# Attention values of two heads in 32 rows of one bank place: half the output copies and transposes, and a new table of steps

## The chip, the cores and the metric

The kernel runs on one core of one Trainium2 chip. The metric is the device time of one launch in microseconds (us). TensorE is written PE in the profile (PEld is its queue of weight loads), VectorE is DVE, ScalarE is ACT, GpSimd is POOL, SyncE is SP.

## The reference, cut to what matters

Two transformer layers over 32 sequences of 256 tokens and 128 channels, all in float32. Each layer is adaptive layer norm, attention with 16 heads of 8 channels, residual, adaptive layer norm, and a mixture of 16 experts of which each token takes two.

```python
h = _layernorm(x) * (1 + ca) + sa
q, k, v = ...                         # 16 heads of 8 channels
scores = q @ k^T / sqrt(8)            # layer 0: + slopes * dist
attn = softmax(scores)
ctx = attn @ v                        # (32, 16, 256, 8) -> (32, 256, 128)
x = x + ga * (ctx @ Wo)
h = _layernorm(x) * (1 + cb) + sb
x = x + gb * experts(h)               # top 2 of 16; layer 1: + a shared expert
```

## The kernel before

**Units and steps.** A unit is one sequence in one layer; there are 64 (32 of layer 0, then 32 of layer 1). The program is one software pipeline over steps, and a new unit enters every 16 steps. Everything a unit needs is placed at a fixed step after the unit's start: `at(step, after)` gives the unit whose step `after` this is. Each engine's program is the same loop over steps (from -44 to about 1280), and within a step it issues what its `if` lines say, in the order of the code. There is no scheduler: each engine's queue is strictly this order, and semaphores do the rest. The last unit enters at step 1008; what follows is the tail.

**A step.** In each step PE computes one head of scores twice: query by key into `ps_s` (L1161, two matmuls), of which DVE takes the row maxima (`mx`, L1553), and key by query into `ps_st` (L1167, two matmuls), of which ACT takes the exponential into `prob` (L821). The first runs at a unit's steps 0 to 15, the second at 26 to 41, with the maxima folded in as extra rows. Both score banks are double: PE's scores of a step wait for DVE's maxima and ACT's exponential of two steps earlier. `prob` holds 8 heads.

**Jobs.** After the scores, PE does at most one or two jobs of `JOBS`, the table of what uses the two banks `ps_job`. Its key is the step modulo 16 (called the place of the step below), and the key's parity is the bank. Before a job, PE waits (`free_bank`) until the last job in that bank has been taken out by DVE or ACT:

```python
for s in range(step - 2, step - 2 * H, -2):
    if standing(s):
        for name, u in standing(s):
            done, value = taken(name, u)
            pe.wait_ge(done, value)
        break
```

**Values.** `av0` to `av3` (`probs_values`, L1032) each take four heads: for each head and each half of the keys, a matmul with the 32 columns of `v_ext` as weights (8 values, a column of ones for the softmax's sum, 23 zeros) and 256 columns of `prob` moving, into rows 32i to 32i+31 of the bank. ACT copies each result of 128 x 256 to `o_sb` (`take_o`, L754). Then `o_t0` and `o_t1` (`out_transpose`, L1040), one for each half of the tokens, transpose four 128 x 128 blocks each, and DVE (`normalise`) takes the reciprocals of the sums (L1372) and multiplies (L1376) into `ctx_sb`. `ctx_t` transposes that, `wo` projects it (L1083), DVE multiplies by the gate (`att_tmp`, L1575), POOL adds it to `x`, DVE and POOL do the second norm (`norm_stats`, `rstd`, `norm_middle` L1342, `norm_rows` L1354), `h2_t` transposes, and `router` (L1097) gives the logits, of which DVE takes the best two (`top_two`).

**Pieces of the experts.** The rows of eight units (a group) are scattered by expert to DRAM by POOL. They are taken in 12 quads of four blocks: transpose (L983), gate and up (L1000, L1001), 10 steps after its start the transpose of the activation (L1013), and 15 after it the down projection (L1020). `QUAD` holds the start step of each: three quads in every 32 steps. POOL gathers the results (`GATHER`) and DVE, ACT and POOL combine them (`COMBINE`).

## Time and profile before

| | us |
|---|---|
| median of 3 runs | 1867.87 (1864.94 to 1874.45) |
| the profiled execution's own time | 1869.03 |
| its span | 1867.3 |
| PE busy | 1491.6 (80%) |
| DVE busy | 1315.7 (70%) |
| ACT busy | 1157.5 (62%) |
| POOL busy | 1028.7 (55%) |
| mean granted clock of PE | 0.911 of full |

A busy share of the whole span mixes stages. The steps of the scores run from about 49 to 1517 us; before is setup, behind is the tail, where no scores are left. In the views, PE is the matmul's own span and PEld the queue from which it is fed, in the program's order, so the start of a job's first weight load and the start of the next thing's first weight load bound the queue time of that job. "Idle before" is the idle time of the engine ahead of an instruction and what ended it. "issue" means nothing that the profile shows was waited for.

### The profile page before, as it was taken

What the parts mean: (1) busy time and instruction counts of PE and PEld (TensorE: products, weight loads), DVE (VectorE), ACT (ScalarE), POOL (GpSimd) and SP (SyncE); (2) the same over time, 40 slices, a digit from 0 to 9 for tenths busy, and PEclk for the clock granted to TensorE, in tenths of its full rate; (3) what the DMA queues carried; (4) which work ended last, traced back from release to release, by engine and by line L of the source; (5) the groups of instructions that cost most, each with busy time, mean ns of one, the idle gap of its engine ahead of it and who ended that gap; (6) DMA issues with size and microseconds to landing.
All of it is one profiled execution on the core that took longest, in us unless ns stands there. A gap on an engine that the chain in (4) does not pass through costs nothing.

```text
span 1867.3 us, 44529 instructions
## 1 busy us (share of the span) xinstructions
PE 1491.6 (80%) x13810; PEld 911.5 (49%) x13810; DVE 1315.7 (70%) x3981; ACT 1157.5 (62%) x2692; POOL 1028.7 (55%) x1411
## 2 busy tenths in 40 slices
PE   2779888889999888899999989998999887435540
PEld 1334444445555555555555555555555555435530
DVE  5669988978888877798888888887788765202110
ACT  1478877877777676677776767766776654113320
POOL 1223335634553766567764767565755556546736
PEclk9989999999999898899999999999999999667665
DMA  6774444445555554455554545555455433224432
GB/s 197 172 205 109 110 103 116 114 122 126 134 130 120 138 132 114 119 127 140 134 137 109 134 122 144 130 124 116 125 134 129 116 87 83 75 80 132 121 93 62
DMA packets 381606, 229.44 MB, mean 123 GB/s; under 512 B 28847, under 2 KB 370161, under 8 KB 380867
## 3 DMA queue, kind: packets, MB, share of 16 engines
q1 hardware_dynamic: 352675, 186.72, 41.4%
q0 software_dynamic: 16384, 33.59, 6.4%
q10 hardware_dynamic: 12320, 6.29, 1.2%
q8 instruction: 120, 1.97, 0.5%
q14 instruction: 107, 0.88, 0.2%
HBM read 122.44 MB, written 103.98 MB: 121 GB/s over the span
## 4 chain that ended last, share of the span: by engine, by line
PE 36%; POOL 20%; DVE 18%; issue 16%; another core or an unknown queue 4%; ACT 4%; DMA 2%; SPq 1%; POOLq 0%; DVEq 0%; ACTq 0%
DVE mx L1553 8%; PE ps_s L1161 7%; POOL y_in L642 7%; PE ps_job L1032 6%; PE ps_q L1020 3%; PE ps_q L1001 3%; POOL slot_dram L625 3%; PE ps_q L983 2%; POOL qk_part L669 2%; POOL y_two L677 2%; POOL qk_rest L665 2%; PE ps_job L1135 2%; PE ps_job L1127 2%; PE ps_q L1013 2%
## 5 line engine op out<-in xcount | busy, mean ns | idle before, releaser
L1553 DVE TENSOR_REDUCE mx<-ps_s 128x2 f32<-128x512 f32 x1024 | 688.2, 681 | 150.3 <-PE ps_s L1161 123.7
L821 ACT ACTIVATE prob<-ps_st 128x512 f32<-128x512 f32 x1024 | 598.9, 593 | 111.1 <-PE ps_st L1167 82.6
L1161 PE MATMUL ps_s<-k_stk,q_stk 51*128 51x256 bf16 x2048 | 403.4, 284 | 79.5 <-DVE mx L1553 37.2
L1167 PE MATMUL ps_st<-q_stk,k_stk 53*128 53x256 bf16 x2048 | 400.2, 281 | 0.8 <-ACT prob L821 0.8
L642 POOL DMA_INDIRECT y_in<-y_dram,slot x256 | 252.4, 986 | 106.7 <-issue 54.6
L1032 PE MATMUL ps_job<-prob,v_ext 128*32 128x256 f32 x4096 | 287.8, 400 | 25.6 <-issue 17.6
L625 POOL DMA_INDIRECT slot_dram<-h_row,slot x256 | 260.6, 1018 | 69.8 <-issue 65.1
L1161 PEld LDWEIGHTS ps_s<-k_stk,q_stk 51*128 51x128 bf16 x2048 | 118.3, 95 | 333.8 <-issue 182.7
L754 ACT ACTIVATE o_sb<-ps_job 128x256 f32<-128x256 f32 x256 | 97.1, 379 | 190.3 <-PE ps_job L1032 127.0
L1032 PEld LDWEIGHTS ps_job<-prob,v_ext 128*32 128x32 f32 x4096 | 115.1, 112 | 133.4 <-issue 54.4
L665 POOL TENSOR_TENSOR qk_rest<-qk_f,qk_part 128x512 f32<-128x512 f32 x64 | 73.9, 1154 | 187.3 <-ACT qk_part L852 187.3
L589 POOL TENSOR_SCALAR ln_ve<-ln_mv 128x2 f32<-128x2 f32 x128 | 28.6, 224 | 225.1 <-DVE ln_mv L1335 219.2
L1541 DVE SCALAR_TENSOR_TENSOR y_two<-y_in,w_top,y_two 128x128 f32<-128x128 f32 x128 | 47.5, 408 | 119.5 <-ACT y_two L736 113.2
L1001 PE MATMUL ps_q<-wgu,h_blk_t 128*128 x640 | 113.1, 310 | 14.8 <-ACT h_blk_t L775 9.7
L1167 PEld LDWEIGHTS ps_st<-q_stk,k_stk 53*128 53x128 bf16 x2048 | 117.0, 95 | 7.9 <-issue 3.8
L1001 PEld LDWEIGHTS ps_q<-wgu,h_blk_t 128*128 128x128 f32 x640 | 95.3, 204 | 24.3 <-issue 22.4
L669 POOL TENSOR_TENSOR qk_part<-qk_rest,qk_part 128x512 bf16<-128x512 f32 x64 | 75.1, 1174 | 53.7 <-ACT qk_part L856 53.0
L983 PE MATMUL ps_q<-ident,h_blk 128*128 128x128 f32 x352 | 66.5, 319 | 43.5 <-issue 30.1
L736 ACT ACTIVATE y_two<-y_in,w_top 128x128 f32<-128x128 f32 x128 | 43.8, 389 | 92.5 <-DMA y_in<-y_dram,slot 58.4
L591 POOL TENSOR_TENSOR ln_rs<-ln_ve,neg_half 128x2 f32<-128x2 f32 x128 | 92.0, 719 | 10.7
L1020 PE MATMUL ps_q<-wd,act_t 128*128 x640 | 97.0, 298 | 0.0
L1020 PEld LDWEIGHTS ps_q<-wd,act_t 128*128 128x128 f32 x640 | 82.8, 202 | 15.0 <-issue 14.7
(206 smaller groups left out, 2919.0 us busy)
## 6 DMA issues: line engine op xcount, KB each, us to landing
part_dram<-qk_part SPq DMA_DIRECT2D x128, 192.0 KB
q_stk<-part_dram SPq DMA_DIRECT2D x128, 192.0 KB
k_stk<-part_dram SPq DMA_DIRECT2D x128, 192.0 KB
h_blk<-slot_dram SPq DMA_DIRECT2D x88, 256.0 KB
y_dram<-y_sb SPq DMA_DIRECT2D x80, 256.0 KB
part_dram<-qk_part SPq DMA_DIRECT2D x128, 128.0 KB
mod_in<-row_dram SPq DMA_DIRECT2D x64, 192.0 KB
part_dram<-qk_part SPq DMA_DIRECT2D x128, 64.0 KB
```

Source lines behind the costliest of these rows:

```text
L625: pool.indirect_dma_start(slot_dram[u.group % 2], bass.IndirectOffsetOnAxis(ap=slot[u.group][:, i:i + 1], axis=0), h2_row[u.no % len(h2_ro ...
L642: pool.indirect_dma_start(y_in[u.par][:, j // 2, j % 2, :], None, y_dram[u.group % 3], bass.IndirectOffsetOnAxis(ap=slot[u.group][:, i:i + ...
L665: pool.tensor_tensor(qk_rest[:], qk_f[:], qk_part[:, 0, :], ALU.subtract).then_inc(qk_r, 1)
L669: pool.tensor_tensor(qk_part[:, 2, :], qk_rest[:], qk_part[:, 1, :], ALU.subtract).then_inc(qk_lo, 1)
L821: sc.activation(prob[:, (k ^ 1) % 8, :], ps_st[k % 2][:], ACT.Exp).then_inc(exp_done, 1)
L983: mm = pe.transpose(ps_lane[q.bank][:, j * P:(j + 1) * P], h_blk[q.blk][:, j * D:(j + 1) * D], ident[:])
L1001: mm = pe.matmul(b[:, j * P:(j + 1) * P], h_blk_t[q.lane][:, j * P:(j + 1) * P], wgu[q.layer][:, w], start=q.layer == 1, stop=True)
L1020: mm = pe.matmul(ps_lane[q.bank][:, j * P:(j + 1) * P], act_t[q.lane][:, j * P:(j + 1) * P], wd[q.layer][:, bass.ds(expert[q.bank][j], P)] ...
L1032: mm = pe.matmul(columns(f"av{g}")[32 * i:32 * i + 32, 0:S], v_ext[u.par][:, kt, h, :], prob[:, h % 8, kt * S:(kt + 1) * S], start=kt == 0 ...
L1161: mm = pe.matmul(ps_s[j % 2][:, t * S:(t + 1) * S], q_stk[us.tri][r0:r0 + R_BIAS, hp, t * P:(t + 1) * P], k_stk[us.tri][r0:r0 + R_BIAS, hp ...
L1167: mm = pe.matmul(ps_st[k % 2][:, t * S:(t + 1) * S], k_stk[ut.tri][r1:r1 + R_MAX, hp, t * P:(t + 1) * P], q_stk[ut.tri][r1:r1 + R_MAX, hp, ...
L1553: dve.tensor_reduce(mx[:, hp // 4, :, 4 * par + hp % 4], ps_s[j % 2][:].rearrange("p (t s) -> p t s", s=S), AX_X, ALU.max).then_inc(max_do ...
```

## The change

1. `v_ext` holds the even head of a pair in columns 0 to 8 and the odd one in 16 to 24 of its 32 columns, with zeros elsewhere. `av0` and `av1` go to the same 128 x 256 place of bank 0 and are accumulated there (`start` only with `av0`, `stop` only with `av1`), and so are `av2` and `av3`. The number of value matmuls stays at 32 in a unit. The columns of the weights `wv`, `bv` and the rows of `wo` are permuted to match.
2. ACT makes two copies in a unit in place of four. `av0` and `av2` have no reader of their own, so `taken` gives None for them and `av1` and `av3` wait for no bank.
3. One job `o_t` with four transposes replaces `o_t0` and `o_t1` with four each; `normalise` is one reciprocal of 128 x 32 and one multiply of 128 x 256.
4. `prob` holds 10 heads in place of 8.
5. Steps: `av0` 32 to 34, `av2` 40 to 42, `wo` 58 to 56, `router` 74 to 72, and what hangs on them: the add to `x` 60 to 58, the second norm's statistics 62 to 60, its power 63 to 61, middle 65 to 64, rows 68 to 66, the top two 74 to 72, `one_hot` 76 to 78, tanh 77 to 76, weights 80 to 81, `count_seen` 78 to 80. Quads start at 190 + (0, 10, 18) in place of 195 + (0, 11, 21) steps after their group's last unit, and the combination of most groups one step later.

```diff
         else:
             first, apart, lag = END + (124, 176, 248)[g - TAIL + 1] + 4 * i, 1, 6
         for j in range(2 * TT):
             GATHER[first + apart * j] = (g * G + i, j)
         COMBINE[first + lag] = g * G + i
     for i in range(NQ):
-        QUAD[last + 195 + 32 * (i // 3) + (0, 11, 21)[i % 3] if g < TAIL else END + (92 if g == TAIL else 164) + 6 * i] = g * NQ + i
+        QUAD[last + 190 + 32 * (i // 3) + (0, 10, 18)[i % 3] if g < TAIL else END + (92 if g == TAIL else 164) + 6 * i] = g * NQ + i
 STEPS = max(COMBINE) + 8
...
-JOBS = {0: [("av0", 32, 0)], 1: [("sh1", 81, 0)], 2: [("o_t1", 50, 0)], 4: [("av1", 36, 0)],
-        5: [("h_t", -27, 0), ("ctx_t", 53, S)], 6: [("max_t1", 22, 0), ("h2_t", 70, S)],
-        7: [("rank", 87, 0), ("owner", 103, P), ("sh_dn", 87, S)], 8: [("av2", 40, 0)], 9: [("qk", -23, 0)],
-        10: [("wo", 58, 0), ("router", 74, S)], 11: [("sh0", 75, 0)], 12: [("av3", 44, 0)],
-        14: [("max_t0", 14, 0), ("v", 14, S)], 15: [("o_t0", 47, 0)]}
+
+JOBS = {1: [("sh1", 81, 0)], 2: [("av0", 34, 0)], 4: [("av1", 36, 0)], 5: [("h_t", -27, 0), ("ctx_t", 53, S)],
+        6: [("max_t1", 22, 0), ("h2_t", 70, S)], 7: [("rank", 87, 0), ("owner", 103, P), ("sh_dn", 87, S)],
+        8: [("wo", 56, 0), ("router", 72, S)], 9: [("qk", -23, 0)], 10: [("av2", 42, 0)], 11: [("sh0", 75, 0)],
+        12: [("av3", 44, 0)], 14: [("max_t0", 14, 0), ("v", 14, S)], 15: [("o_t", 47, 0)]}
 AT = {name: after for jobs in JOBS.values() for name, after, _ in jobs}
 COLUMN = {name: column for jobs in JOBS.values() for name, _, column in jobs}
 BANK = {name: k % 2 for k, jobs in JOBS.items() for name, _, _ in jobs}
...
-        prob = sb("prob", [P, 8, 2 * S])
-        o_sb = [sb(f"o_sb{i}", [P, H // 4, S]) for i in range(2)]
-        den_r = sb("den_r", [P, TT, H])
+        prob = sb("prob", [P, PROBS, 2 * S])
+        o_sb = [sb(f"o_sb{i}", [P, 2, S]) for i in range(2)]
+        den_r = sb("den_r", [P, TT * H])
...
-            def take_o(u, g):
-                sc.wait_ge(av_mm, u.count(4, g + 1))
-                if g == 0 and u.has(2):
-                    sc.wait_ge(ot_mm, u.count(2, -2))
-                sc.activation(o_sb[u.par][:, g, :], ps_job[BANK[f"av{g}"]][:, 0:S], ACT.Copy).then_inc(o_ok, 1)
+            def take_o(u, r):
+
+                sc.wait_ge(av_mm, u.count(4, 2 * r + 2))
+                if r == 0 and u.has(2):
+                    sc.wait_ge(ot_mm, u.count(1, -1))
+                sc.activation(o_sb[u.par][:, r, :], ps_job[BANK[f"av{2 * r + 1}"]][:, 0:S], ACT.Copy).then_inc(o_ok, 1)
             def take_qk(u):
...
                 if u:
                     sc.wait_ge(st_mm, u.count(16, k + 1))
-                    if k >= 8:
-                        sc.wait_ge(av_mm, u.count(4, (k - 8) // 4 + 1))
-                    elif u.has(1):
-                        sc.wait_ge(av_mm, u.count(4, (k + 8) // 4 - 3))
-                    sc.activation(prob[:, (k ^ 1) % 8, :], ps_st[k % 2][:], ACT.Exp).then_inc(exp_done, 1)
-                for g in range(H // 4):
-                    u = at(step, AT[f"av{g}"])
+                    head = u.no * H + (k ^ 1)
+                    if head >= PROBS:
+                        sc.wait_ge(av_mm, (head - PROBS) // 4 + 1)
+                    sc.activation(prob[:, head % PROBS, :], ps_st[k % 2][:], ACT.Exp).then_inc(exp_done, 1)
+                for r in range(2):
+                    u = at(step, AT[f"av{2 * r + 1}"])
                     if u:
-                        take_o(u, g)
+                        take_o(u, r)
                 q = quad_at(step, 0)
                 if q:
                     take_blocks(q)
...
                         sc.wait_ge(dve_const, 5)
-                    sc.activation(v_ext[u.par][:, :, :, 0:DH],
-                                  ps_job[BANK["v"]][:, S:2 * S].rearrange("p (t h d) -> p t h d", t=TT, h=H),
+                    sc.activation(v_ext[u.par][:].rearrange("p t (s b) (c w) -> p (t s) (b c) w", b=2, w=VW // 2)[:, :, 0::3, 0:DH],
+                                  ps_job[BANK["v"]][:, S:2 * S].rearrange("p (s b d) -> p s b d", b=2, d=DH),
                                   ACT.Copy).then_inc(v_ok, 1)
                 u = at(step, AT["ctx_t"])
...
             def taken(name, u):
                 return {"h_t": (h_ok, u.no + 1), "max_t0": (mxt_ok, u.count(2, 1)), "max_t1": (mxt_ok, u.count(2, 2)),
-                        "qk": (qk_ok, u.count(2, 2)), "o_t0": (ctx_norm, u.count(4, 2)), "o_t1": (ctx_norm, u.count(4, 4)),
-                        "av0": (o_ok, u.count(4, 1)), "av1": (o_ok, u.count(4, 2)), "av2": (o_ok, u.count(4, 3)),
-                        "av3": (o_ok, u.count(4, 4)),
+                        "qk": (qk_ok, u.count(2, 2)), "o_t": (ctx_norm, u.count(2, 2)),
+                        "av0": None, "av1": (o_ok, u.count(2, 1)), "av2": None, "av3": (o_ok, u.count(2, 2)),
                         "rank": (plan_step, u.group * PLAN + 1) if u.last else (rank_step, u.count(2, 1)),
                         "v": (v_ok, u.no + 1), "ctx_t": (ctx_ok, u.no + 1), "wo": (att_scaled, u.no + 1),
...
                     if standing(s):
                         for name, u in standing(s):
-                            done, value = taken(name, u)
-                            pe.wait_ge(done, value)
+                            if taken(name, u):
+                                pe.wait_ge(*taken(name, u))
                         break
             def columns(name):
...
                 pe.wait_ge(exp_done, u.count(16, 4 * g + 4))
                 if g == 0:
                     pe.wait_ge(v_ok, u.count(1, 1))
+                r, b = divmod(g, 2)
                 for kt in range(TT):
                     for i in range(4):
-                        h = 4 * g + i
-                        mm = pe.matmul(columns(f"av{g}")[32 * i:32 * i + 32, 0:S], v_ext[u.par][:, kt, h, :],
-                                       prob[:, h % 8, kt * S:(kt + 1) * S], start=kt == 0,
-                                       stop=kt == TT - 1, skip_group_check=True)
+                        mm = pe.matmul(columns(f"av{g}")[32 * i:32 * i + 32, 0:S], v_ext[u.par][:, kt, 8 * r + 2 * i + b, :],
+                                       prob[:, (u.no * H + 4 * g + i) % PROBS, kt * S:(kt + 1) * S], start=b == 0 and kt == 0,
+                                       stop=b == 1 and kt == TT - 1, skip_group_check=True)
                 mm.then_inc(av_mm, 1)
-            def out_transpose(u, t):
-                pe.wait_ge(o_ok, u.count(4, 4))
-                for g in range(H // 4):
-                    mm = pe.transpose(columns(f"o_t{t}")[:, g * P:(g + 1) * P], o_sb[u.par][:, g, t * P:(t + 1) * P], ident[:])
+            def out_transpose(u):
+                pe.wait_ge(o_ok, u.count(2, 2))
+                for t in range(TT):
+                    for r in range(2):
+                        mm = pe.transpose(columns("o_t")[:, (2 * t + r) * P:(2 * t + r + 1) * P],
+                                          o_sb[u.par][:, r, t * P:(t + 1) * P], ident[:])
                 mm.then_inc(ot_mm, 1)
...
-            def normalise(u, t):
-
-                dve.wait_ge(ot_mm, u.count(2, t + 1))
-                o = ps_job[BANK[f"o_t{t}"]][:].rearrange("p (h v) -> p h v", v=VW)
-                dve.reciprocal(den_r[:, t, :].rearrange("p (h o) -> p h o", o=1), o[:, :, DH:DH + 1]).then_inc(ctx_norm, 1)
-                dve.wait_ge(ctx_norm, u.count(4, 2 * t + 1))
-                if t == 0 and u.has(1):
+            def normalise(u):
+
+                dve.wait_ge(ot_mm, u.no + 1)
+                o = ps_job[BANK["o_t"]][:].rearrange("p (h w) -> p h w", w=VW // 2)
+                den = den_r[:].rearrange("p (h o) -> p h o", o=1)
+                dve.reciprocal(den, o[:, :, DH:DH + 1]).then_inc(ctx_norm, 1)
+                dve.wait_ge(ctx_norm, u.count(2, 1))
+                if u.has(1):
                     dve.wait_ge(h_ctx_mm, ctx_turn(u) - 1)
-                dve.tensor_tensor(ctx_sb[:, t, :].rearrange("p (h d) -> p h d", d=DH), o[:, :, 0:DH],
-                                  den_r[:, t, :].rearrange("p (h o) -> p h o", o=1).broadcast_to([P, H, DH]), ALU.mult)\
-                   .then_inc(ctx_norm, 1)
+                dve.tensor_tensor(ctx_sb[:].rearrange("p t (h d) -> p (t h) d", d=DH), o[:, :, 0:DH],
+                                  den.broadcast_to([P, TT * H, DH]), ALU.mult).then_inc(ctx_norm, 1)
             def top_two(u, part):
...
```

**The order around the projection and the next values.** PE, a unit of layer 0 without quads, from the router's matmuls (L1097; L1099 in the changed file) to the next value job of the younger unit (L1032); L1161 and L1167 (L1163 and L1169) are the scores. Before:

```order
L1097 MATMUL ps_job<-wr,h_t 128x16 x2
L1161 MATMUL ps_s<-k_stk,q_stk 128x256
L1167 MATMUL ps_st<-q_stk,k_stk 128x256
L1161 MATMUL ps_s<-k_stk,q_stk 128x256
L1167 MATMUL ps_st<-q_stk,k_stk 128x256
L1161 MATMUL ps_s<-k_stk,q_stk 128x256
L1167 MATMUL ps_st<-q_stk,k_stk 128x256
L1161 MATMUL ps_s<-k_stk,q_stk 128x256
L1167 MATMUL ps_st<-q_stk,k_stk 128x256
L1032 MATMUL ps_job<-prob,v_ext 32x256 x8
```

Now:

```order
L1099 MATMUL ps_job<-wr,h_t 128x16 x2
L1163 MATMUL ps_s<-k_stk,q_stk 128x256
L1169 MATMUL ps_st<-q_stk,k_stk 128x256
L1163 MATMUL ps_s<-k_stk,q_stk 128x256
L1169 MATMUL ps_st<-q_stk,k_stk 128x256
L1055 MATMUL ps_job<-h_t,wq 128x256
L1056 MATMUL ps_job<-h_t,wk 128x256
L1163 MATMUL ps_s<-k_stk,q_stk 128x256
L1169 MATMUL ps_st<-q_stk,k_stk 128x256
L1163 MATMUL ps_s<-k_stk,q_stk 128x256
L1169 MATMUL ps_st<-q_stk,k_stk 128x256
L1032 MATMUL ps_job<-prob,v_ext 32x256 x8
```

Before, the step between the router and the values that wait for its bank held scores alone; now the projections of query and key (L1055, L1056) stand in it.

**The order around the normalisation.** DVE, the same part of the program, from the maxima behind the output transposes on (L1553; L1556 in the changed file): L1372 and L1376 (L1376 and L1380) normalise, L1364 and L1366 (L1367 and L1369) split the maxima, L1425 (L1428) makes the weights of the top two, L1342 and L1354 (L1345 and L1357) are the middle and the rows of the second norm. Before:

```order
L1553 TENSOR_REDUCE mx<-ps_s 128x2
L1372 RECIPROCAL den_r<-ps_job 128x16
L1376 TENSOR_TENSOR ctx_sb<-ps_job,den_r 128x128
L1553 TENSOR_REDUCE mx<-ps_s 128x2
L1364 CAST mx_part<-mx 128x2x8
L1366 TENSOR_TENSOR mx_part<-mx,mx_part 128x2x8
L1425 TENSOR_SCALAR w_top<-dz_th 128x2 x2
L1553 TENSOR_REDUCE mx<-ps_s 128x2
L1342 SCALAR_TENSOR_TENSOR h_mid<-x,ln_mv,mod_in 128x128 x2
L1553 TENSOR_REDUCE mx<-ps_s 128x2
L1372 RECIPROCAL den_r<-ps_job 128x16
L1376 TENSOR_TENSOR ctx_sb<-ps_job,den_r 128x128
```

Now:

```order
L1556 TENSOR_REDUCE mx<-ps_s 128x2
L1376 RECIPROCAL den_r<-ps_job 128x32
L1380 TENSOR_TENSOR ctx_sb<-ps_job,den_r 128x256
L1556 TENSOR_REDUCE mx<-ps_s 128x2
L1367 CAST mx_part<-mx 128x2x8
L1369 TENSOR_TENSOR mx_part<-mx,mx_part 128x2x8
L1345 SCALAR_TENSOR_TENSOR h_mid<-x,ln_mv,mod_in 128x128 x2
L1556 TENSOR_REDUCE mx<-ps_s 128x2
L1428 TENSOR_SCALAR w_top<-dz_th 128x2 x2
L1556 TENSOR_REDUCE mx<-ps_s 128x2
L1357 SCALAR_TENSOR_TENSOR h_row<-h_mid,ln_rs,mod_in 128x128 x2
L1556 TENSOR_REDUCE mx<-ps_s 128x2 x3
```

Two normalisations of half size have become one, and the middle and the rows of the second norm now stand one step earlier, behind the same split of the maxima and on both sides of the weights.

## Rows read from the trace of the kernel before

**Rows 1.** Busy PE, PEld, DVE, ACT, POOL in five stages (us); PE clock, DMA share, GB/s.

```profile
118.00:251.00 133.00, 118.92 (x1338) 62.44 (x1338) 120.72 (x386) 112.59 (x262) 44.77 (x85) 1.00 0.48 110
251.00:550.00 299.00, 265.61 (x2754) 149.66 (x2755) 253.78 (x782) 225.96 (x523) 153.23 (x227) 0.97 0.52 123
550.00:840.00 290.00, 258.13 (x2450) 152.90 (x2450) 232.52 (x676) 202.75 (x472) 172.16 (x237) 0.91 0.51 123
840.00:1516.50 676.50, 617.75 (x5828) 381.59 (x5826) 559.49 (x1698) 474.57 (x1116) 430.98 (x578) 0.97 0.52 127
1516.50:1867.30 350.80, 170.26 (x1060) 137.41 (x1058) 79.36 (x271) 99.89 (x231) 204.43 (x238) 0.70 0.33 91
```

**Rows 2.** Groups by shape: busy us, mean ns of one, idle before and releasers.

```profile
L1553 DVE TENSOR_REDUCE mx<-ps_s 128x2 f32<-128x512 f32 x1024 | 688.2, 681 | 150.3 <-PE ps_s L1161 123.7 <-remote 17.8 <-issue 4.1
...
L754 ACT ACTIVATE o_sb<-ps_job 128x256 f32<-128x256 f32 x256 | 97.1, 379 | 190.3 <-PE ps_job L1032 127.0 <-remote 61.9 <-issue 0.7
...
L1040 PE MATMUL ps_job<-ident,o_sb 128*128 128x128 f32 x512 | 83.6, 287 | 0.7 <-DVE sh_act L1522 0.4 <-ACT o_sb L754 0.3
...
L1354 DVE SCALAR_TENSOR_TENSOR h_row<-h_mid,ln_rs,mod_in 128x128 f32<-128x128 f32 x128 | 44.5, 389 | 0.0
...
L1376 DVE TENSOR_TENSOR ctx_sb<-ps_job,den_r 128x128 f32<-128x128 f32 x128 | 37.3, 291 | 4.4
...
L1372 DVE RECIPROCAL den_r<-ps_job 128x16 f32<-128x16 f32 x128 | 31.9, 249 | 19.2 <-PE ps_job L1040 13.9 <-issue 5.2
...
L1575 DVE TENSOR_TENSOR att_tmp<-ps_job,mod_in 128x256 f32<-128x256 f32 x64 | 26.7, 418 | 15.6 <-PE ps_job L1097 15.4
```

**Rows 3.** PE's weight loads in time: a job of scores, transposes, values, transposes behind a quad.

```profile
163.69 0.09 PEld L1161 LDWEIGHTS ps_s<-k_stk,q_stk 51*128 51x128 bf16 x1 [0.17 <-issue]
...
164.02 0.10 PEld L1046 LDWEIGHTS ps_job<-ident_b,mx_part 128*16 128x16 bf16 x2 [0.21 <-issue]
...
173.54 0.42 PEld L1040 LDWEIGHTS ps_job<-ident,o_sb 128*128 128x128 f32 x4 [0.21 <-issue]
174.12 0.09 PEld L1161 LDWEIGHTS ps_s<-k_stk,q_stk 51*128 51x128 bf16 x1 [0.17 <-issue]
...
174.53 0.62 PEld L1032 LDWEIGHTS ps_job<-prob,v_ext 128*32 128x32 f32 x16 [0.29 <-ACT mx_t L717]
175.56 0.09 PEld L1161 LDWEIGHTS ps_s<-k_stk,q_stk 51*128 51x128 bf16 x1 [0.41 <-issue]
...
903.60 0.47 PEld L1040 LDWEIGHTS ps_job<-ident,o_sb 128*128 128x128 f32 x4
904.24 0.09 PEld L1161 LDWEIGHTS ps_s<-k_stk,q_stk 51*128 51x128 bf16 x1 [0.17 <-issue]
```

**Rows 4.** What PE's weight loads waited for, whole span: us in total, times, longest.

```profile
PEld ps_s L1161 <- DVE mx L1553: 127.8, 248, 2.5
...
PEld ps_job L1032 <- DVE att_tmp L1575: 22.7, 27, 1.0
...
PEld ps_job L1032 <- DVE ctx_sb L1376: 8.6, 22, 0.7
...
PEld ps_job L1032 <- DVE den_r L1372: 4.2, 8, 1.5
```

**Rows 5.** The same from 118 to 251 us.

```profile
PEld ps_s L1161 <- DVE mx L1553: 19.3, 41, 0.8
...
PEld ps_job L1032 <- DVE att_tmp L1575: 6.4, 8, 0.9
```

**Rows 6.** One wait for the gate, in PE's weight loads.

```profile
170.77 0.62 PEld L1032 LDWEIGHTS ps_job<-prob,v_ext 128*32 128x32 f32 x16 [0.87 <-DVE att_tmp L1575]
```

**Rows 7.** Engines over places 15 to 3 of a unit without quads (columns of rows 1).

```profile
173.21:178.00 4.79, 4.01 (x45) 1.94 (x44) 4.69 (x18) 4.49 (x13) 2.48 (x5) 1.00 0.52 152
```

**Rows 8.** POOL's last scatter of a group, and SyncE's load of its first quad.

```profile
1370.21 0.98 POOL L625 DMA_INDIRECT slot_dram<-h_row,slot  x1 [0.30 <-issue]
...
1389.27 0.44 SPq L499 DMA_DIRECT2D h_blk<-slot_dram  x1
```

56 lines of the change are left out of this document (29 added, 27 removed).

## Prediction

> **What bounds the kernel now.** I read the stages first. In the stages with scores PE is busy 89% of the time without quads (118.9 of 133 us), 89% in layer 0 with quads (265.6 of 299 and 258.1 of 290) and 91% in layer 1 (617.8 of 676.5) [rows 1]. DVE is the second: 91% of the first of these stages, 85%, 80%, and 83% in layer 1. ACT stands at 85% down to 70%, POOL and the DMA queues lower. The last 350.8 us are the tail, with PE and DVE far from busy; the change leaves it nearly as it is, and I count nothing there. From the profile's start of the scores at about 49 us to 1516.5 us there are 63 intervals between units, so 23.3 us on the mean; the stage from 118 to 251 us holds 8 units of 16.6 us, each with 16 steps.
>
> Then the waits of PE's queue. It waits most for DVE's maxima: 127.8 us in 248 waits; 22.7 us are for DVE's gate multiplication before a value job, and 12.8 us (8.6 and 4.2) for the normalisation before the next one [rows 4]. So PE sets the time, and DVE pulls it up where steps hold little for PE: in the first stage PE waits 19.3 us for maxima, 2.4 us in a unit, and DVE is idle only (133 - 120.7) / 8 = 1.5 us in a unit [rows 5, 1]. The reader sees it best over the places 15, 0, 1, 2 and 3 of one such unit: DVE is busy 4.69 of 4.79 us there, PE 4.01 [rows 7]. What leaves PE's queue is gain in full where PE is the only bound, and in part where DVE stands right behind it.
>
> **The sum.** It is made against the profiled execution, 1869.0 us, which is 1.2 us over the median shown; I neglect that.
>
> *Transposes of outputs.* Now 512 of them in 128 jobs of four, then 256 in 64 jobs [rows 2]. A job takes from its first weight load to that of the next scores 0.58 us (173.54 to 174.12), and 0.64 us behind a quad's piece (903.60 to 904.24) [rows 3]. With 0.60 us, 64 jobs are **38 us** of PE's queue, all of it on PE's path. The mean of 287 ns in the group is the span of one, of which four overlap, and isn't to be multiplied.
>
> *The wait for the normalisation.* `av1` stood two steps behind `o_t1` in the same bank and waited for it, 12.8 us in 30 waits [rows 4]. Now it waits for no bank, and the next user of the bank of `o_t` stands two steps behind in layer 1 (`sh1`) and six in layer 0 (`ctx_t`). I take **13 us** off; the bound on the other side is 0, where `sh1` inherits the wait.
>
> *The wait for the gate.* `av3` waited for the multiplication of `wo` and for the top two out of the same bank, 22.7 us in 27 waits, one of them 0.87 us; 6.4 us of them lie in 8 units of the first stage [rows 4 to 6]. In layer 0 the step between held scores alone. Now `av2` waits for it, with the projection of query and key in between, as the first place of the order shows, and that job gives DVE the time it lacks. I take **23 us** off; the bounds are 0 and 23.
>
> *Values.* 32 matmuls a unit before and after, of the same shape. Nothing on PE. The zeros that the second head adds cost what the first's padding cost.
>
> *ACT.* 128 of 256 copies at 379 ns are 48.5 us [rows 2]. ACT is nowhere above 85%, so this is cover, not gain: PE and DVE already hide it, and without that cover it would be paid. `max_t1` still stands two steps behind `av1` and its copy, so no wait for these copies goes either. The copy of values into `v_ext` has two more strides and the same size; nothing.
>
> *DVE.* Two reciprocals and two multiplications (249 + 291 ns twice, 1.08 us) become one of each. The multiplication of 128 x 256 is like `att_tmp`, 418 ns; for the reciprocal of 32 I take 265 ns, 249 and 1 ns for each of 16 more elements, which is the step from 291 to 418 ns over 128 elements [rows 2]. That saves 0.40 us a unit, 25 us in all, of DVE's work. It shortens what PE waits for, and I count it in the give-back below. The Trainium skill ("VectorE: DVE Perf Modes", section on the trn2 errata) gives 120 cycles and one per element at 0.96 GHz for a read from PSUM, by which a reciprocal of 16 would take 142 ns and the merging would save 0.25 us; the rows have 249 ns for it, so their larger fixed part is used.
>
> *Steps.* Ten heads in `prob` let two of the four refills of a unit wait for values four steps back, and two for values two steps back as all did; no row shows PE held by this, and I count nothing. `wo` three steps behind `ctx_t` in place of five, and `router` two steps behind `h2_t` in place of four, keep the two steps that PE's bank waits had anyway. The second norm has a step more for POOL's power and a step less from middle to rows, and `h2_t` stands four steps behind the rows in place of two. Quads start five steps earlier: the last scatter is issued at 1370.2 us and the load of the first quad at 1389.3 us, 19 us later [rows 8]. Five steps at 1.6 us take 8 us of that, so it stays hidden; if the 11 us left were too few, SyncE would stand in its queue, and the loads of maxima behind it. No DMA is added or removed.
>
> *What DVE gives back.* The three terms are 74 us, some 1.8 us a unit in layer 0 (0.60, 0.84 and 0.4) and 0.75 in layer 1. At places 15 to 3 of a unit without quads PE now has five times 0.33 us of scores, 0.58 of transposes and 1.03 of values, 3.3 us, where it had 3.8 [rows 3]. DVE has its 4.69 us [rows 7], less 0.40, and the rows of the second norm, which the second place of the order shows moved in (two at 389 ns [rows 2]): 5.1 us. There the transposes removed give nothing, and what I gain is the two bank waits. In the 12 units without quads, where DVE has 1.5 us idle and 0.4 us saved in a unit, I count a third: 12 x 0.6 = 7 us. In the 20 units of layer 0 with quads, whose pieces now fall on places 0, 1, 2, 3 and 15, half: 20 x 0.9 = 18 us. In the 32 units of layer 1, where the shared expert fills place 1, two thirds: 32 x 0.5 = 16 us. That is 41 us: 1869 - 41 = **1828 us**. The shares are a judgement; their bounds are all of it, 1869 - 74 = 1795 us, and a quarter, 1869 - 18 = 1851 us.
>
> **The rivals.**
>
> *All of it shows.* The pieces of quads fill the steps that held scores alone so well that PE's waits for maxima do not grow, or fall. For it: those waits are 127.8 us, more than the three terms. Against it: the first stage, where DVE is at 91%. 1795 to about 1810 us, taken as 1800.
>
> *DVE is the bound already.* PE's freed time turns into waits for maxima nearly everywhere. For it: DVE busy for 98% of the places that hold the transposes [rows 7]. Against it: 17% of idle time of DVE in layer 1, over half of the span with scores. A quarter or less is left: 1851 to 1869, taken as 1860 us.
>
> *The crowded steps stall (slower).* At places 15 to 3 DVE's 5.1 us stand against PE's 3.3, an excess of 1.8 us; before it was 4.69 less 3.8, 0.9 us [rows 3, 7]. If this growth of 0.9 us came as a stall in each of the 64 units, and the two bank waits came back as waits for maxima behind it, it would be 58 us against 38 us: 1889 us. It decides from 38 / 64 = 0.6 us a unit. For it: DVE is full at these places already [rows 7]. Against it: in 52 of 64 units quads or the shared expert put more work for PE there.
>
> *PE's clock (slower).* The granted clock is 1.00 in the first stage, 0.97 in layer 1, and 0.91 from 550 to 840 us, where PE waits more [rows 1]; full is 2.4 GHz, and half of it, 1.2 GHz, is the other level. If less work on PE brought the stages at 0.97 to 0.91 too, 0.06 of 299 and 676.5 us, 58 us of full-rate time, would go, and 91% of it would be PE's: 53 us, for 1881 us. Against it: the drops lie where PE waits, not where it has few jobs; the stage without quads has the fewest jobs and the full clock. The Trainium skill ("TensorE: Matmul & The Clock Gate", Part 1) says that activity releases the throttle and idleness brings it back; by that the removed jobs speak for this rival and the removed waits against it.
>
> *It does not do what it says.* If the values were spread over more matmuls, or the second head restarted the place, the counts would show it; the order has eight matmuls in a value job as before, so no chance is given.
>
> **How the numbers follow.** A difference of 0.5% (9.3 us) is about what a measurement of this kernel can tell from none. Forecast (1812 to 1850): 0.58. All of it: 0.22. DVE the bound: 0.13, nearly all within 0.5%. Crowded steps 0.05, clock 0.02. Faster by more than 0.5%: 0.58 + 0.22, and 0.01 of the third: 0.81; same 0.12; slower 0.07. The range of 8 in 10 leaves out the slower rivals, half of the third and the lower end of "all of it": 1798 to 1858 us.
>
> **What would show it.** Right: 256 records of output transposes, 128 copies at about 379 ns, a normalising pair of about 265 and 418 ns; no wait of L1032 for the normalisation and almost none for the gate; units of the first stage at about 16.0 us, of layer 1 about half a microsecond shorter; waits of PE for maxima at 130 to 160 us. Wrong: a stage from 118 us on that is no shorter with DVE over 95% busy (DVE the bound); waits for maxima of over 180 us in all, with those behind the transposes about 2 us a unit (crowded steps); a clock of 0.93 or less in layer 1; a wait of PE for a quad's load (scatters too late); or a wait of `sh1` for the normalisation.

## The result and the profile after

The changed kernel takes 1943.99 us (median of 4 runs, 1933.04 to 1946.54), where before takes 1867.7 us beside it: a ratio of 1.0395 [1.0359, 1.0431], slower by 76 us. The forecast was 1828 us, with 7 in 100 for slower; its time and its sign are wrong. The profiled execution has a span of 1944.7 us and a mean granted clock of 0.875.

Page of the kernel after, busy us of each engine with its share of the span:

```profile
PE 1508.0 (78%) x13554; PEld 916.8 (47%) x13554; DVE 1331.2 (68%) x3853; ACT 1118.5 (58%) x2564; POOL 1033.5 (53%) x1411
```

PE has its 256 matmuls less and DVE its 128 operations less, and both are busy longer, not shorter: PE by 16 us and DVE by 16 us.

Windows of the kernel after by stage: window and its us, busy us (instructions) of PE, PEld, DVE, ACT, POOL, PE's granted clock, DMA share, GB/s. The scores run to 1598 us, before to 1516.5:

```profile
118.00:251.00 133.00, 115.81 (x1236) 57.22 (x1236) 119.40 (x348) 103.29 (x236) 44.46 (x84) 0.94 0.46 103
251.00:550.00 299.00, 261.20 (x2691) 143.44 (x2691) 258.50 (x760) 215.12 (x491) 149.66 (x223) 0.93 0.50 120
550.00:840.00 290.00, 242.05 (x2309) 145.38 (x2305) 214.75 (x616) 186.38 (x430) 161.49 (x223) 0.89 0.50 120
840.00:1598.00 758.00, 663.97 (x5940) 412.30 (x5936) 594.00 (x1707) 477.51 (x1103) 452.50 (x602) 0.90 0.49 117
1598.00:1944.70 346.70, 164.78 (x1031) 131.85 (x1030) 76.54 (x262) 97.58 (x225) 203.11 (x236) 0.71 0.33 92
```

Against [rows 1], the tail is as long as it was (346.7 us, 350.8 before) and the clock is lower in every stage with scores: 0.94, 0.93, 0.89, 0.90 where it was 1.00, 0.97, 0.91, 0.97. I count a unit from the first weight load of its scores to that of the next. Unit 4 begins at 126.0 us, unit 28 at 605.5 and unit 63 at 1572.1 (before 124.1, 591.3 and 1493.1): a unit takes 19.98 us up to the 28th and 27.61 us behind it, where it took 19.46 and 25.77. So 24 x 0.52 = 12 us come from the first part, and 35 x 1.84 = 64 us, most of the loss, from the part in which layer 1's units overlap the combination of expert results.

Waits of the kernel after (engine, line, releaser: us in total, times, longest), of PE's queue and POOL, and below them the view of SyncE's queue:

```profile
PEld ps_s L1163 <- DVE mx L1556: 201.3, 311, 3.0
...
POOL y_two L678 <- DMA gate_b<-row_dram: 92.9, 31, 5.4
...
PEld ps_job L1129 <- DVE ctx_sb L1380: 5.3, 10, 0.6
...
PEld ps_job L1032 <- DVE att_tmp L1577: 3.2, 3, 1.3
```

```profile
SPq L478 <- PE ps_st L1169: 368.9, 58, 12.0
...
SPq L467 <- POOL qk_part L670: 155.0, 45, 6.7
```

The two bank waits that were to go have gone: the value jobs wait 3.2 us for the gate's multiplication (22.7 before [rows 4]), and not at all for the normalisation, of which the shared expert's second job (L1129) took over 8.3 us: 5.3 for the multiplication and 3.0 for the reciprocal (1.5 in all before). But PE waits 201.3 us for maxima in place of 127.8. And there is a wait that before does not have at all: in 31 combinations POOL waits for the load of `gate_b`, 92.9 us in all. PE also waits 30.0 us for the loads of quads, where it waited 11.7, which the forecast had named as a sign of scatters that come too late; e6 below looks at it. SyncE waits 155.0 us for POOL's last piece of query and key, where the like row of before has this:

```profile
SPq L466 <- POOL qk_part L669: 64.6, 40, 4.2
```

Groups of instructions of the kernel after, shapes apart (busy us, mean ns):

```profile
L1345 DVE SCALAR_TENSOR_TENSOR h_mid<-x,ln_mv,mod_in 128x128 f32<-128x128 f32 x128 | 58.7, 499 | 6.8 <-POOL ln_rs L592 5.8 <-issue 0.3
...
L756 ACT ACTIVATE o_sb<-ps_job 128x256 f32<-128x256 f32 x128 | 49.1, 384 | 74.2 <-PE ps_job L1032 41.6 <-remote 29.9
...
L1041 PE MATMUL ps_job<-ident,o_sb 128*128 128x128 f32 x256 | 42.8, 292 | 0.0
...
L1412 DVE TENSOR_TENSOR hot<-idx,iota_e 128x64 bf16<-128x64 uint32 x64 | 38.9, 608 | 0.0
...
L1380 DVE TENSOR_TENSOR ctx_sb<-ps_job,den_r 128x256 f32<-128x256 f32 x64 | 27.2, 424 | 2.2
...
L1376 DVE RECIPROCAL den_r<-ps_job 128x32 f32<-128x32 f32 x64 | 22.4, 349 | 19.2 <-PE ps_job L1041 13.3 <-issue 5.8
```

Counts and shapes are those that the forecast's sum had. Two operations that the change only moves have become longer: the one-hot (`hot`) and the first of the normalisation (`h_mid`). The same groups before:

```profile
L1342 DVE SCALAR_TENSOR_TENSOR h_mid<-x,ln_mv,mod_in 128x128 f32<-128x128 f32 x128 | 44.3, 386 | 24.9 <-POOL ln_rs L591 24.6
...
L1409 DVE TENSOR_TENSOR hot<-idx,iota_e 128x64 bf16<-128x64 uint32 x64 | 23.3, 364 | 0.0
```

**Where the gate load went.** The timeline of SyncE's queue before, around one combination:

```profile
982.62 0.50 SPq L554 DMA_DIRECT2D gate_b<-row_dram  x1
...
989.80 0.84 SPq L481 DMA_DIRECT2D q_stk<-part_dram  x2
```

And of SyncE and POOL in the kernel after:

```profile
1007.66 0.85 SPq L482 DMA_DIRECT2D q_stk<-part_dram  x2
...
1008.56 1.18 SPq L482 DMA_DIRECT2D k_stk<-part_dram  x2
...
1009.78 0.47 SPq L555 DMA_DIRECT2D gate_b<-row_dram  x1
...
1014.28 0.73 POOL L678 TENSOR_TENSOR y_two<-y_two,gate_b 128x256 f32<-128x256 f32 x1 [2.25 <-DMA gate_b<-row_dram]
...
1018.16 1.15 POOL L670 TENSOR_TENSOR qk_part<-qk_rest,qk_part 128x512 bf16<-128x512 f32 x1
...
1019.33 0.90 SPq L467 DMA_DIRECT2D part_dram<-qk_part  x2
```

The diff has one number for it: `lag` from 13 to 14. The load of `gate_b` is issued six steps ahead of the combination (`done_at(step, -6)`), so it moved from place 3 to place 4. At place 4, ahead of it in the same queue, stands `stack_rows` of another unit, which waits until the scores of three units back are through (L478, 368.9 us in 58 waits). So the load now comes some 9 us later against that queue's other work: before, 7.2 us ahead of the first load of the stacks (989.80 less 982.62); now 2.1 us behind it (1009.78 less 1007.66). POOL multiplies by the gate in order, and behind that multiplication stand `ln_rs`, the last piece of query and key, and through it SyncE's stores (L467).

**What slowed DVE.** Timeline of DVE, POOL and PE's queue after, in a unit without quads:

```profile
193.84 1.16 POOL L670 TENSOR_TENSOR qk_part<-qk_rest,qk_part 128x512 bf16<-128x512 f32 x1
193.87 1.21 DVE L1412 TENSOR_TENSOR hot<-idx,iota_e 128x64 bf16<-128x64 uint32 x1
...
195.94 0.09 PEld L1163 LDWEIGHTS ps_s<-k_stk,q_stk 51*128 51x128 bf16 x1 [1.51 <-DVE mx L1556]
...
197.27 0.09 PEld L1163 LDWEIGHTS ps_s<-k_stk,q_stk 51*128 51x128 bf16 x1 [1.21 <-DVE mx L1556]
...
197.64 1.93 PE L1032 MATMUL ps_job<-prob,v_ext 128*32 128x256 f32 x16
...
199.50 0.10 PEld L1163 LDWEIGHTS ps_s<-k_stk,q_stk 51*128 51x128 bf16 x1 [0.81 <-DVE mx L1556]
```

The one-hot, moved from step 76 to 78, now falls on place 14, where POOL makes that last piece. It begins 0.03 us behind POOL's operation and ends 0.08 us behind its end. The other one-hots of this profile bear it out: the 15 of 64 with no elementwise operation of POOL beside them take 213 to 220 ns. Of the 42 that begin during one, 33 end 0.08 us (within 0.03) behind the end of an operation of POOL, and nine are not held and take 214 to 218 ns. PE then waits 1.51, 1.21 and 0.81 us for maxima. Behind the first two waits the granted clock falls from 1.00 to 0.50, which is 1.2 GHz (columns as in the windows above):

```profile
196.00:197.00 1.00, 0.34 (x4) 0.06 (x4) 0.97 (x3) 0.88 (x2) 0.00 (x0) 1.00 0.34 115
198.00:199.00 1.00, 1.00 (x16) 0.39 (x8) 1.00 (x5) 0.37 (x1) 0.00 (x0) 0.50 1.14 337
```

The value job there takes 1.93 us. Before, at the full clock, one takes 1.07:

```profile
174.56 1.07 PE L1032 MATMUL ps_job<-prob,v_ext 128*32 128x256 f32 x16
```

The Trainium skill ("SBUF — State Buffer", Who interferes with whom) says that a DVE instruction with two SBUF inputs contends with a GpSimd instruction that reads SBUF, and that the port pair they share is an exclusive lock; by that rule the one-hot is held until POOL's 1.16 us are over. These two rows agree in that the end of POOL's operation sets that of the one-hot; but only 0.08 us lie between the two ends, where a one-hot alone takes 0.21 us.

### The profile page after: what moved, and what is told of

Read it like the earlier page. It is cut to its first block, busy times and chain, and to the rows that moved or that the text cites. A ratio compares the mean times of both kernels' runs of the same rounds, so it can differ in the third digit from the quotient of the medians.

```text
span 1944.7 us, 43565 instructions
## 1 busy us (share of the span) xinstructions
PE 1508.0 (78%) x13554; PEld 916.8 (47%) x13554; DVE 1331.2 (68%) x3853; ACT 1118.5 (58%) x2564; POOL 1033.5 (53%) x1411
## 4 chain that ended last, share of the span: by engine, by line
PE 45%; DVE 14%; POOL 10%; issue 10%; DMA 8%; another core or an unknown queue 5%; SPq 4%; ACT 3%; POOLq 0%; ACTq 0%; DVEq 0%
PE ps_s L1163 10%; PE ps_job L1032 8%; DVE mx L1556 6%; POOL y_in L643 5%; DMA gate_b<-row_dram 4%; PE ps_q L1001 3%; PE ps_q L1020 3%; SPq L482 3%; PE ps_job L1137 2%; PE ps_q L1013 2%; DMA h_blk<-slot_dram 2%; PE ps_job L1085 2%; PE ps_q L983 2%; PE ps_job L1129 2%
## 5 line engine op out<-in xcount | busy, mean ns | idle before, releaser
L1556 DVE TENSOR_REDUCE mx<-ps_s 128x2 f32<-128x512 f32 x1024 | 687.9, 683 | 211.3 <-PE ps_s L1163 185.6
L1163 PE MATMUL ps_s<-k_stk,q_stk 51*128 51x256 bf16 x2048 | 406.4, 290 | 117.1 <-DVE mx L1556 76.4
L1169 PE MATMUL ps_st<-q_stk,k_stk 53*128 53x256 bf16 x2048 | 402.9, 288 | 1.0 <-issue 0.7
L1032 PE MATMUL ps_job<-prob,v_ext 128*32 128x256 f32 x4096 | 306.6, 420 | 3.8 <-issue 1.9
L1163 PEld LDWEIGHTS ps_s<-k_stk,q_stk 51*128 51x128 bf16 x2048 | 122.9, 96 | 376.9 <-DVE mx L1556 201.3
L1032 PEld LDWEIGHTS ps_job<-prob,v_ext 128*32 128x32 f32 x4096 | 114.5, 116 | 117.2 <-issue 75.6
L666 POOL TENSOR_TENSOR qk_rest<-qk_f,qk_part 128x512 f32<-128x512 f32 x64 | 74.7, 1167 | 142.9 <-ACT qk_part L853 142.9
L1001 PE MATMUL ps_q<-wgu,h_blk_t 128*128 x640 | 118.5, 320 | 12.6 <-ACT h_blk_t L777 7.5
L1169 PEld LDWEIGHTS ps_st<-q_stk,k_stk 53*128 53x128 bf16 x2048 | 121.5, 96 | 10.5 <-issue 4.9
L1001 PEld LDWEIGHTS ps_q<-wgu,h_blk_t 128*128 128x128 f32 x640 | 100.3, 213 | 23.2 <-issue 20.6
L678 POOL TENSOR_TENSOR y_two<-y_two,gate_b 128x256 f32<-128x256 f32 x64 | 47.1, 736 | 119.4 <-DMA gate_b<-row_dram 92.9
L1020 PE MATMUL ps_q<-wd,act_t 128*128 x640 | 103.9, 312 | 0.0
L1020 PEld LDWEIGHTS ps_q<-wd,act_t 128*128 128x128 f32 x640 | 88.9, 215 | 16.5 <-issue 16.3
L756 ACT ACTIVATE o_sb<-ps_job 128x256 f32<-128x256 f32 x128 | 49.1, 384 | 74.2 <-PE ps_job L1032 41.6
```

Source lines behind the costliest of these rows:

```text
L666: pool.tensor_tensor(qk_rest[:], qk_f[:], qk_part[:, 0, :], ALU.subtract).then_inc(qk_r, 1)
L1001: mm = pe.matmul(b[:, j * P:(j + 1) * P], h_blk_t[q.lane][:, j * P:(j + 1) * P], wgu[q.layer][:, w], start=q.layer == 1, stop=True)
L1020: mm = pe.matmul(ps_lane[q.bank][:, j * P:(j + 1) * P], act_t[q.lane][:, j * P:(j + 1) * P], wd[q.layer][:, bass.ds(expert[q.bank][j], P)] ...
L1032: mm = pe.matmul(columns(f"av{g}")[32 * i:32 * i + 32, 0:S], v_ext[u.par][:, kt, 8 * r + 2 * i + b, :], prob[:, (u.no * H + 4 * g + i) % P ...
L1163: mm = pe.matmul(ps_s[j % 2][:, t * S:(t + 1) * S], q_stk[us.tri][r0:r0 + R_BIAS, hp, t * P:(t + 1) * P], k_stk[us.tri][r0:r0 + R_BIAS, hp ...
L1169: mm = pe.matmul(ps_st[k % 2][:, t * S:(t + 1) * S], k_stk[ut.tri][r1:r1 + R_MAX, hp, t * P:(t + 1) * P], q_stk[ut.tri][r1:r1 + R_MAX, hp, ...
```

## The experiments

There were 18 runs of 16 kernels on several chips, each beside runs of before on its own chip; I compare ratios. Before took 1866.8, 1884.6 and 1885.7 us beside the first twelve (four each), and 1775.9 us beside e13 to e16 and 1777.1 beside e17 and e18. I call these conditions A and B. Nothing on record ties them to a chip: the runs of e9 to e12 (A) and those of e13 to e16 (B) carry the same chip number. The difference turned out to matter, and comes last.

### Single moves of the change undone

Each kernel is the change with one edit: the combination a step earlier as before; the gate load alone a step earlier; the one-hot at 76; the second normalisation's two operations where they were.

```diff
e1_lag13
-            first, apart, lag = last + 332 + H * i, 2, 14
+            first, apart, lag = last + 332 + H * i, 2, 13
e2_gate_load
-                u = done_at(step, -6)
+                u = done_at(step, -7)
e3_one_hot
-                u = at(step, 78)
+                u = at(step, 76)
                 if u:
                     one_hot(u)
e4_norm
norm_middle: at(step, 64) -> at(step, 65)
norm_rows:   at(step, 66) -> at(step, 68)
```

> The changed kernel with the combination one step earlier again (13 steps behind the first gather, as before), so that SyncE loads the gate at place 3, ahead of the stacks' loads at place 4, and POOL and DVE combine where they did. Late gate (the load of gate_b stands behind the stacks' wait in SyncE's queue, POOL waits 92.9 us for it in 31 waits, and the splits of query and key behind it come late): the wait is gone, layer 1 falls from 28.0 us a unit to about 26.0, the whole to 1880-1895 us. Crowded steps or the shared port of DVE and POOL as the cause: 1935-1945 us, as the changed kernel.

> The changed kernel with SyncE's load of the gate one step earlier (place 3) and nothing else moved. Late gate, by SyncE's queue alone: as the kernel with the combination moved back, 1880-1895 us, POOL's wait for gate_b under 10 us. If it is the place of the combination on POOL, DVE and ACT that costs, and not the load: 1925-1945 us.

> The changed kernel with DVE's one-hot back at step 76 (place 12) in place of 78 (place 14, where POOL runs the split of query and key for 1.17 us). DVE held by POOL: hot falls from 608 ns to 250-360 ns, units 4 to 11 from 17.9 to about 16.8 us, the whole by 15-30 us to 1915-1930 us. Late gate as the only cause: the whole within 6 us of 1944 us, and units 4 to 11 unchanged.

> The changed kernel with the second norm's middle and rows at steps 65 and 68 again (places 1 and 4) in place of 64 and 66 (places 0 and 2). Crowded steps: the waits of PE for maxima fall by 40 us or more from 201 us, the whole to 1905-1930 us. Late gate or shared port as the causes: 1935-1945 us.

| kernel | us | ratio to before |
|---|---|---|
| e1_lag13 | 1927.86 | 1.0323 [1.0254, 1.0392] |
| e2_gate_load | 1910.73 | 1.0242 [1.0178, 1.0306] |
| e3_one_hot | 1930.29 | 1.0358 [1.0287, 1.0429] |
| e4_norm | 1950.43 | 1.0430 [1.0356, 1.0505] |

The gate load alone takes back 1.5%. Its 1910.73 us lie between the ranges of its two theories (1880 to 1895, 1925 to 1945). Its kernel has no wait of POOL for the gate, and SyncE's wait for POOL's piece is down to this:

```profile
SPq L467 <- POOL qk_part L670: 90.9, 39, 7.3
```

Its units are at 19.97 us up to the 28th, as in the change, and 26.50 us behind it (27.61 in the change): it acts where there are combinations. The whole combination a step earlier takes away the same waits (88.5 us left of SyncE's) and gives less, 0.7%, with overlapping intervals; it too lies between its ranges. The one-hot alone is within the interval of the change, but its profile shows the other part of the loss healed. Group of the one-hot and windows in that kernel:

```profile
L1412 DVE TENSOR_TENSOR hot<-idx,iota_e 128x64 bf16<-128x64 uint32 x64 | 17.0, 265 | 0.0
```

```profile
118.00:251.00 133.00, 118.33 (x1329) 60.68 (x1327) 122.36 (x383) 109.53 (x250) 45.94 (x89) 0.99 0.49 111
840.00:1400.00 560.00, 491.43 (x4460) 306.33 (x4460) 435.70 (x1281) 358.65 (x832) 346.36 (x463) 0.92 0.51 120
```

In the first stage PE does 1329 matmuls in the 133 us, where the change does 1236, at a clock of 0.99, where it is 0.94: a unit takes 18.91 us up to the 28th, which is less than before's 19.46, and units 4 to 11 take 16.4 us (17.9 in the change, 16.8 expected). Behind it is no better than the change (27.40 us). The normalisation put back gives nothing (1950 us, where a gain to 1930 or less was the theory's sign), so the crowding of DVE by its rows, the heart of my slower rival, is not what cost.

### Both together, the quads, and the transposes twice

```diff
e5_gate_hot: e2_gate_load and e3_one_hot together
e6_quads: the change with
-        QUAD[last + 190 + 32 * (i // 3) + (0, 10, 18)[i % 3]
+        QUAD[last + 195 + 32 * (i // 3) + (0, 11, 21)[i % 3]
e7_gate_hot_quads: e5 and e6 together
e8_twice: e7, and in out_transpose
-                for t in range(TT):
+                for t in (0, 1, 0, 1):
```

> The changed kernel with the gate's load at place 3 and the one-hot at step 76 together. Alone they gave 33 and 14 us against 1944. If both are causes and independent (one in layer 1, the other before the combinations begin): 1890-1900 us. If the queues only wait for the next late thing: above 1908 us.

> The changed kernel with the starts of the quads as before (195 and 0, 11, 21 in place of 190 and 0, 10, 18). PE idles 60 us before quads' transposes for their loads, where it idled 24 us before. Late loads of quads as a third cause: 10-25 us faster than 1944 us, nothing changed before 270 us. Else within 6 us, or slower, since the pieces leave the places 0 to 3 that hold little for PE.

> Gate's load, one-hot and quads' starts all back. If the three are what costs, the values in one place then show what they are worth: at or under 1867 us (the kernel before). If the crowded places 15 to 3 or the clock still cost: 1875-1895 us.

> As the run with all three back, but PE does its four transposes of outputs twice into the same place, so that PE has as many of them as before the change (256 more). If PE's queue is the bound: 25-38 us slower than that run. If DVE and the waits set the time at these places: within 10 us. If more activity keeps PE's clock up: granted clock higher by 0.01 or more, and the time no worse.

| kernel | us | ratio to before |
|---|---|---|
| e5_gate_hot | 1899.77 | 1.0061 [1.0035, 1.0088] |
| e6_quads | 1949.29 | 1.0360 [1.0290, 1.0429] |
| e7_gate_hot_quads | 1908.24 | 1.0117 [1.0060, 1.0173] |
| e8_twice | 1910.69 | 1.0129 [1.0081, 1.0176] |

Gate load and one-hot together take back 3.2% of the 3.95% (1.0061 / 1.0395 = 0.968). The 1899.77 us lie in the expected 1890 to 1900, but before took 1884.55 us beside them and not 1867.7, so by the ratio that is more than was expected. The old quad starts give nothing, alone or on top, though alone they bring PE's waits for the loads of quads down from 30.0 to 12.3 us; e7 lies above e5, with intervals that overlap, and its hope of 1867 us or less failed. Page of the first of these kernels:

```profile
PE 1479.2 (78%) x13554; PEld 904.9 (48%) x13554; DVE 1290.7 (68%) x3853; ACT 1113.9 (59%) x2564; POOL 1031.3 (54%) x1411
```

DVE is busy 1290.7 us, 25.0 us under before, in a kernel that is still no faster than before. That is the forecast's 25 us by luck: the normalisation gives 19.7 of them, and the rest comes from slightly shorter maxima, `h_mid` and `y_two`. And PE's transposes, done twice (the same results written twice, 256 more matmuls), cost 2.5 us where 38 were reckoned: 1910.69 against 1908.24 us. Group of the transposes in that kernel:

```profile
L1041 PE MATMUL ps_job<-ident,o_sb 128*128 128x128 f32 x512 | 69.9, 279 | 3.3 <-DVE sh_act L1525 2.5 <-issue 0.2
```

PE's clock went from 0.893 to 0.902 with them, which on PE's 1493 busy us is worth some 15 us (an estimate from the two clocks), and the two intervals leave room for some 16 us of cost. Together that is less than 38. So in condition A the transposes were not all on the path, and by the medians less than half of them. For DVE's saving no such run was made.

### More of the moves undone

On the change with combination and one-hot as before (e9_comb_hot): the first values job back at 32, the weights' step back at 80, and the whole second normalisation with POOL's parts back (60, 62, 63, 65, 68).

```diff
e10_av0
+JOBS = {0: [("av0", 32, 0)], 1: [("sh1", 81, 0)], 4: [("av1", 36, 0)], ...
e11_top
-                u = at(step, 81)
+                u = at(step, 80)
                 if u:
                     top_weights(u)
e12_norm
POOL's sum 58 -> 60, norm_stats 60 -> 62, rstd 61 -> 63, norm_middle 64 -> 65, norm_rows 66 -> 68
```

> The change with its whole combination (its gate load with it) one step earlier, and the one-hot at step 76, both as before. The kernel in which the gate load alone went back (beside the same one-hot) measured 1.0061 of before. Theory: what held the combination was the queue of its gate load, and the step of the combination itself is worth nothing: 1.000 to 1.010 of before (1868 to 1887 us on a chip where before is 1868), GpSimd's waits for the gate gone, VectorE's one-hot at 265 ns. Rival: the units of layer 1 that are still slower than before (26.0 to 26.9 us against 25.5 to 25.9) are so because the combination's x still comes a step late, and the ratio falls below 1.000 and those units to under 25.9 us.

> The kernel before this one, with the first values job moved back from step 34 to 32, where before had it. In all kernels with the change's steps place 2 of layer 1 takes 1.8 to 2.3 us and place 4 2.0 to 2.3 us (before 1.7 at place 4), with the TensorE's clock halved in that stretch. Theory: crowded steps are what is left, two values jobs within three steps of the busiest stretch; with the first at place 0, whose step is now the emptiest (0.5 us against 1.4 before), 5 to 12 us come back. Rival: the sum of the places is what counts, the maxima of VectorE set the pace through all of them, and the time stays within 4 us of the kernel without this edit.

> The kernel with combination and one-hot back, with the weights of the routed heads' choice (two VectorE operations of 0.4 and 0.3 us) moved back from step 81 to 80, as before. Theory of crowded steps: place 1 (1.8 to 2.1 us in layer 1 against 1.6 to 1.9 before) gives back up to 0.3 us a unit, place 0 takes it: within 4 us of the kernel without this edit, either side. Rival: step 80 comes before the shared part's VectorE work at step 81, and what waits for the weights (GpSimd's count and the rank) comes earlier: faster by 4 to 10 us.

> The kernel with combination and one-hot back, with the whole second normalisation back where before had it: GpSimd's sum at step 60 instead of 58, VectorE's moments 62 instead of 60, GpSimd's root 63 instead of 61, VectorE's two normalising operations 65 and 68 instead of 64 and 66; projection stays at 56. GpSimd's sum waits 45 to 49 us in all for the scaled projection in the change. Theory: VectorE's h_mid operation is slowed while GpSimd works (mean 499 ns in the change, 386 before), so that 5 to 10 us come back and the mean of that operation falls to about 386 ns. Rival: the two steps later only shift it, and with the router still at step 72 its rows come too late: slower by 0 to 10 us.

| kernel | us | ratio to before |
|---|---|---|
| e9_comb_hot | 1911.26 | 1.0129 [1.0102, 1.0156] |
| e10_av0 | 1905.04 | 1.0103 [1.0066, 1.0140] |
| e11_top | 1910.64 | 1.0148 [1.0120, 1.0177] |
| e12_norm | 1931.78 | 1.0252 [1.0227, 1.0276] |

All four stay above 1.000. e9 lies above both of its ranges (1.000 to 1.010, or under 1.000): the whole combination a step earlier is no better than its gate load alone. The expectation for the first value job (5 to 12 us) fits with 6 us, but the intervals overlap, so "within 4 us" isn't ruled out. The weights' step does nothing in the median (0.6 us). The normalisation put back costs 1.2%, 20.5 us, twice the most that the rival had: with the router at 72 its rows come late. In the profiles PE waits 10.6 us for them in place of 2.0, which is not all of the cost. No single step explains what is left.

### The sum without the moves, the moves without the sum

The last question was whether the summed values are worth anything by themselves. Three kernels keep before's own values (`prob` with eight buffers, `av0` at 32): e13 with all other moves of the change, e14 with the same but gate load and one-hot mended, and e15 with few moves. e16 has the summed values with the same few moves and ten buffers. The few are those that the sum forces or that go with them: third values job at 42, projection 56, router 72, second normalisation.

```diff
e13_steps: before, with
-        7: [...], 8: [("av2", 40, 0)], 9: [("qk", -23, 0)],
-        10: [("wo", 58, 0), ("router", 74, S)], ...
+        7: [...], 8: [("wo", 56, 0), ("router", 72, S)], 9: [("qk", -23, 0)],
+        10: [("av2", 42, 0)], ...
and all the numbers of the change for normalisation, one_hot, top_weights, count_seen, tanh, lag, QUAD
e14_steps_mended: e13_steps with one_hot at 76 and the gate load at done_at(step, -7)
e15_few_steps: before, with the job table of e13_steps and the change's second normalisation alone
e16_sum_few: the change, with av0 32, lag 13, QUAD 195 and (0, 11, 21), one_hot 76, tanh 77,
             count_seen 78, top_weights 80
```

> The kernel before with its own values (four bank places, eight transposes of outputs, two normalisations), but on the change's steps: third values job at 42, projection 56, router 72, second normalisation, one-hot 78, weights 81, counts 80, tanh 76, combination a step later, quads' starts 190 and 0, 10, 18. Only the first values job stays at 32 and the transposes at 47 and 50; the probabilities keep 8 buffers, so that the next unit's first exponential waits for the values job in its own step. Theory b (the sum is worth something, the moves cost more): slower than the change, 1.05 to 1.065 of before. Theory a (the sum is worth nothing): as the change, 1.035 to 1.045.

> The kernel before this one, with the gate load a step earlier and the one-hot at 76, which on the change gave 1.0061 of before. Theory b: 1.02 to 1.03, and the sum's own gain is this less 1.006. Theory a: 1.000 to 1.010. Both: 0.025 to 0.035 below the kernel before this one, since gate load and one-hot cost the same with either form of the values.

> The kernel before with only those moves that the summed values force or that go with them: third values job at 42, projection 56, router 72, GpSimd's sum 58, moments 60, root 61, normalising operations 64 and 66. Values, one-hot, weights, counts, tanh, combination and quads as before. If the forced moves cost what theory b says: 1.015 to 1.03 of before. If not: 0.995 to 1.005.

> The change with only the forced moves: the summed values at 32, 36, 42 and 44, transposes at 47, projection 56, router 72 and second normalisation as in the change; one-hot 76, weights 80, counts 78, tanh 77, combination and quads as before. Theory b: 0.985 to 0.998 of before if the free moves were what cost, and below the kernel before this one by 0.01 to 0.03. Theory a: 1.005 to 1.015, within 0.005 of the kernel before this one.

| kernel | values | moves | us | ratio to before |
|---|---|---|---|---|
| e13_steps | old | all but `av0` | 1843.40 | 1.0374 [1.0357, 1.0391] |
| e14_steps_mended | old | all but `av0`, two mended | 1782.50 | 1.0039 [1.0023, 1.0055] |
| e15_few_steps | old | few | 1781.57 | 1.0021 [1.0008, 1.0035] |
| e16_sum_few | summed | few | 1741.18 | 0.9805 [0.9785, 0.9825] |

The moves by themselves, with not one instruction of the values changed, cost 3.7%, and gate load and one-hot are 3.2% of it (1.0039 / 1.0374 = 0.968, the factor found with the summed values). All other moves together cost 0.4%. The two were not taken apart here. e14's gain over e13 lies behind the 28th unit (25.56 to 24.28 us a unit; 19.74 to 19.51 before it), which speaks for the gate load; and the one-hot, at 76 again, takes 575 ns in the mean, more than the 434 at 78, since at 76 it now meets POOL's first piece of query and key (L666). The sum by itself gives 0.9805 / 1.0021 = 0.978, 40.4 us, where the forecast's net was 41.

By the expectations e13 and e14 read as theory a, the sum is worth nothing (1.0374 in 1.035 to 1.045, 1.0039 in 1.000 to 1.010). But they set old values in condition B against ratios of the change from A. e16 against e15, both in B, says the opposite, and its 0.9805 is below what either theory had. The pages of e15 and e16, in this order:

```profile
PE 1459.8 (82%) x13810; PEld 890.1 (50%) x13810; DVE 1328.3 (74%) x3981; ACT 1164.0 (65%) x2692; POOL 1030.8 (58%) x1411
```

```profile
PE 1418.7 (82%) x13554; PEld 861.1 (50%) x13554; DVE 1295.3 (74%) x3853; ACT 1125.3 (65%) x2564; POOL 1031.4 (59%) x1411
```

PE is busy 41 us less and DVE 33 us less.

### The same kernels beside each other again

But beside e13 to e16 before itself takes 1776 us, so e16 and e5 were repeated side by side. Both are unchanged. Both runs fell into condition B; e16 was never run in A.

> The kernel with the summed values and only the forced moves once more (0.9805 of before, where before took 1776 us). If the free moves are what took the gain: 0.975 to 0.99 of before again, wherever before stands. If the gain belongs to the conditions in which before takes 1776 us: 1.00 to 1.01 where before takes 1865 to 1890 us, and 0.98 again where it takes 1776.

> The change with gate load and one-hot back once more (1.0061 of before, where before took 1885 us; the same moves on the old values gave 1.0039 where it took 1776). If the free moves are what took the gain: 1.00 to 1.01 again, wherever before stands. If it belongs to the conditions: 0.98 to 0.99 where before takes 1776 us, and 1.006 again where it takes 1865 to 1890.

| kernel | us | ratio to before (1777.06 us) |
|---|---|---|
| e18_sum_few_again | 1740.97 | 0.9795 [0.9772, 0.9817] |
| e17_gate_hot_again | 1748.87 | 0.9833 [0.9806, 0.9859] |

The second of the two expectations holds, not that of the free moves: the very kernel that measured 1.0061 where before takes 1885 us measures 0.9833 where before takes 1777. Against e14 (old values, the same mended moves but `av0` at 32, 1.0039) that is again a gain of 2.1% for the sum. So in condition B the sum has its gain, and in A the same kernel shows none against before. Below, "there" is A and "here" is B. Windows of that kernel there and here, 840 to 1400 us; there first:

```profile
840.00:1400.00 560.00, 497.01 (x4564) 309.78 (x4562) 439.03 (x1307) 366.50 (x855) 355.67 (x480) 0.93 0.51 123
```

```profile
840.00:1400.00 560.00, 531.71 (x5147) 331.18 (x5145) 495.57 (x1482) 414.67 (x963) 389.11 (x521) 0.98 0.58 139
```

In the same 560 us it does 13% more matmuls here, with a clock of 0.98 for 0.93. Up to unit 28 the two stand close (19.25 and 18.84 us a unit); behind it 26.60 and 23.74 us, there and here, and from the start of unit 63 to the end 374.4 and 338.7 us. The maxima last the same in both (683 and 682 ns). What differs is waits that the profile there puts down to nothing on the core (`remote`). Of ACT and DVE there:

```profile
ACT prob L822 <- remote: 48.6, 15, 5.6
...
DVE mx L1556 <- remote: 47.7, 17, 4.2
...
ACT q_stk L803 <- remote: 36.9, 2, 36.6
...
ACT o_sb L756 <- remote: 35.0, 16, 4.4
```

One of them in the timeline:

```profile
879.17 0.28 PE L1163 MATMUL ps_s<-k_stk,q_stk 51*128 51x256 bf16 x1
...
879.49 1.73 PE L1032 MATMUL ps_job<-prob,v_ext 128*32 128x256 f32 x16
...
883.57 0.69 DVE L1556 TENSOR_REDUCE mx<-ps_s 128x2 f32<-128x512 f32 x1 [3.94 <-remote]
883.61 0.60 ACT L822 ACTIVATE prob<-ps_st 128x512 f32<-128x512 f32 x1 [5.13 <-remote]
...
884.32 0.09 PEld L1163 LDWEIGHTS ps_s<-k_stk,q_stk 51*128 51x128 bf16 x1 [3.58 <-DVE mx L1556]
```

The scores that DVE and ACT wait for were issued by 879.2 us and the value job at 879.49, and both engines start at 883.6 us, within 0.04 us of each other; PE then waits for them. In the profile of the same kernel here no wait is put down so, and ACT's waits for PE at the exponential and at the copy are 2.4 and 1.3 us at most:

```profile
ACT prob L822 <- PE ps_st L1169: 160.6, 218, 2.4
...
ACT o_sb L756 <- PE ps_job L1032: 38.4, 90, 1.3
```

Before has them too, where it takes 1867 us (61.9 us in 26 waits of ACT's copy to `o_sb`). These waits go with the condition and not with the kernel: all 14 profiles from A have them (107 to 233 us of ACT and DVE together), and none of the six from B has any. With overlaps counted once they are 96 us in before, which takes 92 us longer there than here (1867.87 and 1775.87 us), and 145 us in e5, which takes 146 us longer (1895.15 and 1748.87 us, the profiled executions). So they have the size of the whole difference, and the changed kernel has 49 us more of them than before, which is more than the sum's gain. That is an argument from two kernels and not shown: among the kernels of A these waits do not rank the times (e10 has 107 us of them and takes 1905 us, e5 has 145 and takes 1900). What stops the engines there stays open too, and no kernel of the old values on mended moves ran in A.

## Why the prediction was wrong

**"Steps", costed at nothing, is the step that failed.** The paragraph asked of each move whether PE's banks would still be free and whether the quads' loads stay hidden. It closed with "No DMA is added or removed". That is true, and it missed the DMA that was moved: with `lag` 14 the load of `gate_b` went from place 3 to place 4, behind `stack_rows` in SyncE's queue. The paragraph does not name the combination at all. It also does not name the one-hot, nor what POOL does at place 14. The two cost 3.2% by two pairs (e5 to the change, e14 to e13), some 60 us; the gate load alone is 1.5%, and the one-hot 1.8% behind it (e2 to e5, on two chips). All other moves were rightly near nothing: 0.4% in e14, which leaves out that of `av0`.

**This is 62 of the 116 us by which the forecast missed.** The cause of the other 54 stays open. With the two mended (e5) the kernel stood at 1.006 of before in condition A, in which the forecast was measured, and not at the forecast's 0.978. So "all of it on PE's path" and the shares that follow did not hold there either: e8 shows the transposes in part off the path, and the waits without a releaser may have taken the rest.

**The sum's own size was right in condition B, in part by luck.** Net 41 us were forecast, and 40.4 us measured between e15 and e16, 2.1% again between e14 and e17. But the 41 hold a share of the 23 us for the gate's wait. That wait is gone in e15 already (4.4 us left), by the moved projection alone, and e15 is no faster than before (1.0021). And between e15 and e16 DVE saves 33 us and not 25, as the one-hot (556 to 252 ns) and `h_mid` (457 to 361 ns) fell too. The sum also has a slip: 1.8 us a unit in layer 0 and 0.75 in layer 1 make 82 us over the 64 units and not the 74 of its three terms; with 74 the same shares would have left some 37 us. The transposes' doubling (e8) was not repeated in B.

**The waits went as said, without their gain.** 22.7 us for the gate's multiplication became 3.2, and of the normalisation's 12.8 us 8.3 went over to `sh1`, which was the lower bound's case.

**DVE's saving was mis-sized by one term and hidden by another.** The reciprocal of 32 takes 349 ns, not 265: 16 more elements cost 100 ns, not 16. The pair costs 773 ns, so a unit saves 0.31 us and not 0.40, 19.7 us in all and not 25. In the change it was hidden by the one-hot (15.6 us more) and `h_mid` (14.4 us more); with gate load and one-hot back (e5) it shows.

**The give-back.** PE's waits for maxima passed the 180 us that I had named as the sign of crowded steps (201.3), but its mechanism, rows of the normalisation moved in, was wrong: with them put back e4 is no faster (1.0430 against 1.0395) and e12 is slower. Maxima wait 185 us in e5 and 178 us in e16, the fastest kernel, too. So that sign does not tell slow from fast; the count of matmuls in a window does.

**The clock rival** had its sign in the profile: 0.90 in layer 1, under the 0.93 named. For the most part the clock follows the waits, as its "against it" had it: with half the transposes gone it is still 0.99 in the first stage of e3, and over the whole it rose with the two late things mended and the same matmuls (0.875 in the change, 0.889 in e5). But the work has a part too: 256 more transposes raised it from 0.893 to 0.902 (e8 against e7). No run prices the clock by itself.

**The chances.** 7 in 100 for slower was too little, since of all the moved numbers of the diff only that of the quads was followed through the queue that issues it.

## What to carry to other kernels

When a step is moved by one place, write down every queue that it touches at the new place and what stands ahead of it there with a wait, DMA issues first; a lag of one step cost 1.5% because a load fell behind another unit's wait. Do the same with operations of VectorE that read two SBUF tensors: look at what GpSimd runs at that place. And when a change couples an arithmetic saving with a new table, build the two halves apart: here e16 keeps the saving (0.98 of before, in condition B) with the old table wherever it fits. Compare ratios only where before itself takes the same time: one kernel stood at 1.006 and at 0.983 of it.

## What was not expected of the hardware

- A one-hot of 128 x 64 from two SBUF tensors takes 0.21 us with no operation of POOL beside it, and 1.21 us when it begins just behind the start of one of 1.16 us that reads SBUF; it then ends 0.08 us behind POOL's. The step alone doesn't tell which: at step 76 the mean is 265 ns in e3, 375 in e5 and 575 in e14, at step 78 it is 608 in the change and 434 in e13.
- A reciprocal from PSUM took 249 ns for 16 columns and 349 ns for 32, so 6 ns for each further one, where a multiplication from PSUM went from 291 to 424 ns over 128 columns, 1 ns each.
- The same kernel took 1899.77 us beside a before of 1885 and 1748.87 us beside one of 1777, with maxima of the same length (683 and 682 ns). The longer one has waits of 2 to 5 us, once a unit in long stretches, in which ACT and DVE start again together.
- 256 more matmuls for transposes cost 2.5 us in 1908 (e8 against e7, condition A), with the intervals overlapping, while the mean clock rose by 0.009.
